# A layer-two expert program placed one edge batch further forward in a graph kernel

## The reference, cut to what matters

```
xn  = layernorm(x)
x   = x + gnn(xn) + attention(xn)       # gnn: two GAT layers, then the second one's result per node
x   = x + ffn(layernorm(x))             # ffn: 8 experts, all used, weighted by a softmax gate

gat: e = leaky_relu(el[src] + er[dst]); a = softmax of e over the edges of each dst
     out[dst] = sum of a * feat[src]
ffn: h = relu(bn(x @ W1[e] + b1)); h = relu(bn(h @ W2[e] + b2)); y = h @ Wo[e] + bo
     out = sum over e of w[e] * y[e]
```

## Time and profile before

| | us |
|---|---|
| median of 3 runs | 3636.33 (3636.3 to 3638.42) |
| the profiled execution | 3636.28 |
| its span, first to last instruction | 3634.4 |
| POOL busy in the span | 2350.2 |
| DVE busy | 2594.4 |
| PE busy | 2213.0 |
| ACT busy | 1905.4 |

### The profile page before, as it was taken

The page is one execution under the profiler, slowest core; times in us unless marked ns, Lnnn a source line. Parts: engine busy times, 40 slices in busy tenths (PEclk is TensorE's granted clock), DMA queues, the critical chain, the costliest instruction groups (busy, mean ns, idle before and its releaser), DMA issues. The chain is left out here.

```text
span 3634.4 us, 37755 instructions
## 1 busy us (share of the span) xinstructions
PE 2213.0 (61%) x8126; PEld 1372.6 (38%) x8126; DVE 2594.4 (71%) x6161; ACT 1905.4 (52%) x6135; POOL 2350.2 (65%) x2057
## 2 busy tenths in 40 slices
PE   5960044444444444544545540079999999999999
PEld 3540022232223223332323320045555555555565
DVE  8987378888888888888865643366666666666742
ACT  1210067777776667666733333256565655555642
POOL 0004788888888888888646547777777777777500
PEclk9985566666665555555567875589999999999999
DMA  6321389999999999999944435766666666666510
GB/s 189 94 74 21 115 316 348 341 342 346 343 347 338 356 371 363 362 358 369 341 156 115 114 79 170 226 196 201 199 202 200 204 201 203 199 199 199 183 44 11
DMA packets 279436, 821.07 MB, mean 226 GB/s; under 512 B 71711, under 2 KB 149135, under 8 KB 257694
## 3 DMA queue, kind: packets, MB, share of 16 engines
q0 software_dynamic: 126496, 377.09, 34.5%
q1 hardware_dynamic: 121790, 420.89, 30.4%
q10 hardware_dynamic: 30944, 20.94, 2.1%
HBM read 425.16 MB, written 394.56 MB: 226 GB/s over the span
## 5 line engine op out<-in xcount | busy, mean ns | idle before, releaser
L1323 POOL DMA_INDIRECT e_rows<-scratch_table,k_src x1680 | 1975.0, 1176 | 514.1 <-issue 345.8
L1435 ACT ACTIVATE e_rows<-e_rows,e_wr 128x64 f32<-128x64 f32 (+1 forms) x4200 | 1202.1, 367 | 3.6
L1415 DVE SCALAR_TENSOR_TENSOR e_ring<-e_ring,e_kext,e_rows 128x512 f32<-128x512 f32 (+1 forms) x1568 | 964.2, 615 | 226.1 <-ACT e_rows L1435 135.9
L2071 PE MATMUL e_p_y<-e_wfo,e_h 128*112 128x256 f32 x1792 | 418.7, 388 | 40.8 <-DVE e_y L1833 40.7
L2057 PE MATMUL e_p_b<-e_h,e_wf 128*128 128x448 f32 x896 | 374.8, 563 | 19.5 <-ACT e_h L1980 19.5
L2071 PEld LDWEIGHTS e_p_y<-e_wfo,e_h 128*112 128x112 f32 x1792 | 321.9, 181 | 152.0 <-ACT e_h L1980 60.7
L2045 PE MATMUL e_p_a<-e_xt,e_wf 128*128 128x448 f32 x896 | 358.7, 544 | 0.7 <-ACT e_xt L1995 0.7
L1980 ACT ACTIVATE e_h<-e_p_a,e_shift,e_scale 128x448 f32<-128x448 f32 x224 | 160.3, 721 | 281.6 <-PE e_p_a L2045 281.6
L978 PE MATMUL e_p_c<-e_vext,e_kphi 112*128 112x129 f32 x224 | 68.1, 458 | 374.5 <-DVE e_kphi L868 374.5
L1833 DVE SCALAR_TENSOR_TENSOR e_y<-e_p_y,e_w,e_y 112x256 f32<-112x256 f32 x448 | 194.3, 475 | 96.5 <-PE e_p_y L2071 96.4
L1383 DVE TENSOR_TENSOR e_rows<-e_rows,e_wr 128x3840 f32<-128x3840 f32 x56 | 232.6, 4153 | 13.5 <-ACT e_wr L1428 13.5
(11 more groups left out here) (393 smaller groups left out, 3763.3 us busy)
## 6 DMA issues: line engine op xcount, KB each, us to landing
scratch_sums<-e_ring SPq DMA_DIRECT2D x56, 2112.0 KB, 9.7
scratch_sums<-e_ring SPq DMA_DIRECT2D x56, 1848.0 KB, 9.4
scratch_sums<-e_ring SPq DMA_DIRECT2D x56, 1032.0 KB, 4.5
scratch_sums<-e_ring SPq DMA_DIRECT2D x56, 903.0 KB
e_rows<-scratch_table,k_src POOLq DMA_INDIRECT x1680, 4.8
scratch_table<-na_frow ACTq DMA_DIRECT2D x56, 227.5 KB, 2.3
scratch_table<-hi_frow ACTq DMA_DIRECT2D x56, 115.5 KB, 2.1
na_x<-in_x SPq DMA_DIRECT2D x7, 896.0 KB, 17.3
```

Source lines behind the costliest of these rows:

```text
L1323: nc.gpsimd.indirect_dma_start(out=rows[:, n % B, g, :], out_offset=None, in_=table, in_offset=bass.IndirectOffsetOnAxis(ap=k.src[:, n * G ...
L1415: nc.vector.scalar_tensor_tensor(ring[:, i, j - c0, 0:W], prev, kext[:, 0, j + 1:j + 2], rows[:, rb, j, 0:W], ALU.mult, ALU.add).then_inc( ...
L1435: last = nc.scalar.activation(rows[:, rb, j, at], rows[:, rb, j, at], ACT.Copy, scale=wr[:, b, h, j + 1:j + 2])
L2071: last = nc.tensor.matmul(self.p_y[bank][0:BK, i * D:(i + 1) * D], self.h2[:, e % 2, kt, v:v + BK], self.wfo[:, e, kt, :], start=kt == 0, ...
```

## The change

In the `Experts` class a constant `AHEAD = 1` is added, and `place(n)` gives (r, kq) of n + 1 instead of n. SyncE, VectorE and ScalarE use it, so each thing that the expert program does stands one batch (15 steps) sooner beside the ring steps. Some are then put at other steps: `below` goes from step 3 to step 11 of kq 2, `shares` to step 14, the joins, `spread` and `norm` to kq 3. Together `below` stands 7 ring steps sooner than before, and `norm` 11. On TensorE `turn(g)` goes behind `second_layer(f, 7)`, and `outputs(f, 6)` ahead of `first_layer(g, 0)`; the tails' matmuls, `turn_weights` and `bias` go one or two experts later. The tails' own steps on the other engines don't move. In GpSimd's order the node gathers of groups 1 to 13 stay; those of group 0 go from batch 8, steps 0 to 7, to batch 6, steps 7 to 14.

```diff
+    AHEAD = 1
+    def place(self, n):
+        return (n + self.AHEAD) // PB, (n + self.AHEAD) % PB
     def sync(self, sp, n, half):
-        r, kq = n // PB, n % PB
+        r, kq = self.place(n)
     def pool(self, pool, n, j):
-        if n % PB == 0 and n >= 2 * PB and j < 2 * KB:
+        if n == PB + 2 and j >= G - 2 * KB:
+            at = j - (G - 2 * KB)
+            self.gather(pool, 0, at // 2, at % 2)
+        if n % PB == 0 and n >= 3 * PB and j < 2 * KB:
             self.gather(pool, n // PB - 2, j // 2, j % 2)
     def vector(self, dve, n, j):
-        r, kq = n // PB, n % PB
+        r, kq = self.place(n)
...
         if kq == 2:
-            if j == 3:
+            if j == 11:
                 self.below(dve, g)
-            if j == 7:
+            if j == 14:
                 self.shares(dve, g)
-            if j in (7, 10, 11, 13):
-                self.join(dve, g, (7, 10, 11, 13).index(j))
-            if j == 14:
+        if kq == 3:
+            if j in (1, 2, 4, 5):
+                self.join(dve, g, (1, 2, 4, 5).index(j))
+            if j == 6:
                 self.spread(dve, g)
-        if kq == 3 and j == 5:
-            self.norm(dve, g)
+            if j == 9:
+                self.norm(dve, g)
     def scalar(self, act, n, j):
-        nc, r, kq = self.nc, n // PB, n % PB
+        nc, (r, kq) = self.nc, self.place(n)
+        if self.valid(g - 1) and kq == 0 and j == 0:
+            self.keep(act, g - 1, 0, 0)
...
-            if kq == 2 and j == 3:
+            if kq == 2 and j == 10:
                 self.weights(act, f)
         if self.valid(g):
-            if kq == 2 and j == 4:
+            if kq == 2 and j == 12:
                 act.wait_ge(self.d_ready, g + 1)
...
-            if kq == 3 and j == 3:
+            if kq == 3 and j == 7:
                 act.wait_ge(self.sd_asked, g + 1)
...
-            if kq == 3 and j == 8:
-                self.turned(act, g, 0)
-                self.turned(act, g, 1)
...
-        if self.valid(g) and kq == 3 and j == 13:
-            self.keep(act, g, 0, 0)
+        if self.valid(g) and kq == 3 and j == 12:
+            self.turned(act, g, 0)
+            self.turned(act, g, 1)
     def tensor(self, pe):
             for e in range(E):
-                if e == 7 and self.valid(g):
-                    self.turn(pe, g)
                 if on and e < E - 1:
                     self.first_layer(pe, f, e + 1)
-                if e == 0 and self.valid(q):
+                if e == 2 and self.valid(q):
                     tails.tensor_turn(pe, q)
-                if e == 1 and self.valid(q):
+                if e == 3 and self.valid(q):
...
-                if e == 2 and 0 <= q < Q - 1:
+                if e == 4 and 0 <= q < Q - 1:
                     tails.tensor_spread(pe, q)
-                if e == 4 and on:
+                if e == 5 and on:
                     self.turn_weights(pe, f)
-                if e == 5 and on:
+                if e == 6 and on:
                     self.bias(pe, f)
                 if on:
                     self.second_layer(pe, f, e)
-                if e == 0 and self.valid(q):
+                if e == 2 and self.valid(q):
                     tails.tensor_back(pe, q)
+                if e == 7 and self.valid(g):
+                    self.turn(pe, g)
+                if e == 0 and self.valid(o):
+                    self.outputs(pe, o, E - 1)
+                if e > 0 and on:
+                    self.outputs(pe, f, e - 1)
                 if e == 7 and self.valid(g):
                     pe.wait_ge(self.xt_ready, 2 * (g + 1))
...
                     self.first_layer(pe, g, 0)
-                if e == 0 and self.valid(o):
-                    self.outputs(pe, o, E - 1)
-                if e > 0 and on:
-                    self.outputs(pe, f, e - 1)
-                if e == 7 and self.valid(g):
                     self.gate(pe, g)
```

## The result

The changed kernel takes 3729.49 us (median of 4 runs, 3728.65 to 3733.34), the kernel before, run beside it, 3637.38 us: a ratio of 1.0253, 95% interval 1.0236 to 1.0271. Predicted were 3726 us, and slower. The profiled execution took 3733.34 us with a span of 3731.6 us, 97.2 us more than the span before. 6.3 us of these lie ahead of layer two (its first edge gather is issued at 2189.40, before at 2183.09), in work that the change doesn't touch; a second profile of the same kernel lacks them (span 3722.4, layer two from 2180.57). From layer two's first gather to the end it is 1542.2 us against 1451.3, so +90.9.

A forecast was written before the change was run, and what follows sets the result against it. It took GpSimd's stream of gathers in layer two to set the pace. Its terms, 2.5 + 83 + 5.9 + 1.5 - 3.0 = +89.9 us, on a median of 3636.33 gave 3726 us, range 3672 to 3748 (chance 0.8).

The forecast's parts named there:

- seven steps in hand: GpSimd's gathers at L: 37 ring steps ahead of VectorE, of 44 allowed without a wait; the change leaves none.
- L: The moment in each round when VectorE, idle at below for the group's last node gather, goes on.
- S: GpSimd's stall per round in layer two: 4.9 us plus 3.3 for the clock, 8.3 us with the semaphore.
- The join block: VectorE's work from below to norm, with 14 ring steps instead of 18: gather 24 stalls 4.2 us.
- TensorE behind it: From turn to first_layer(g,2), its keep and VectorE's step at p = 40: ends at L+46.3, a stall of 4.9 us.
- The clock: TensorE, idle 8 to 9 us before the turn, then runs at the lower clock: 3.3 us per round (bounds 0 and 4).
- Rival 1: TensorE's gap before the turn splits into pieces that don't lower its clock: S = 4.9, 3687 us; chance 0.20.
- What it waits it can't regain: GpSimd from L on: its issues stood back to back, so time spent waiting for VectorE is never made up.
- The bound of 1.5 us: Gathers 10 to 24: a waiting GpSimd meets less VectorE work, sparing at most 1.5 us per round; 0 was taken.
- A longer chain: Steps behind the turn wait for ScalarE's keeps and hold VectorE and GpSimd: S above 9.9, over 3748 us; chance 0.10.
- TensorE as the bound: TensorE sets the round, which would shrink to the 85.0 us that 68 gathers take: 3576 us; chance 0.06.
- Buffers that don't bind: GpSimd is nearer than counted or VectorE's 14 steps are faster: S is 0, no change, 3636 us; chance 0.04.

The follow-up runs named there:

- e6: The changed kernel with AHEAD back at 0 and the tails' matmuls back at their earlier experts; 3627.39 us, 0.9975 of the kernel before.
- e7: The changed kernel with four buffers of edge rows in layer two instead of three; 3694.40 us, 1.0164 of the kernel before.
- e10: The kernel before, with GpSimd's layer-two gathers waiting for a ring step 7 further on than the buffer needs; 3647.14 us, 1.0041 of the kernel before.
- e8: The changed kernel with 40 matmuls of 64 columns on TensorE ahead of the turn, results unused; 3699.82 us, 1.0179 of the kernel before.
- e5: The changed kernel run once more without an edit; 3729.85 us, 1.0261 of the kernel before.
- e12: e6 with 40 matmuls of 64 columns on TensorE ahead of each turn, results unused; 3640.68 us, 1.0019 of the kernel before.
- e9: The changed kernel with both four row buffers in layer two and 40 filler matmuls ahead of the turn; 3665.92 us, 1.0085 of the kernel before.
- e1: The same kernel as e6, run on another chip where the kernel before takes 3824.93 us; 3882.00 us, 1.0142 of it.

## Why the prediction was right

**GpSimd sets the pace, with seven steps in hand at L, and the change takes them.** Right. GpSimd's waits name VectorE's ring step, at L+9 to L+54, and make 105 us, where 80 to 95 were expected. That the batch forward of the expert program causes them, e6 shows (a batch later, and all of it is gone); that these waits are the three buffers' limit, e7 (none over 0.3 us left, though only 3.4 of the 8.4 us a round come back, since the wait for the tails follows); that the seven steps in hand count even where nothing else moves, e10 (1.5 us a round).

**Terms of the sum.**

| the prediction's term | predicted | measured |
|---|---|---|
| 1: group 0 waits for its tails | +2.5 | +1.0 up to L(1) (GpSimd waited 3.0, 0.3 of it issue) |
| 2: ten rounds | +83 | +84.2 (987.63 - 903.41) |
| 3: last gather round, to the end of turn 12 | +5.9 | +7.4 |
| 4: turn 12 to turn 13 | +1.5 | +1.3 |
| 5: behind the last turn | -3.0 | -3.0 (93.91 against 96.91) |
| sum | +89.9 | +90.9 |

**What S is made of.** The sum of S was right (8.3 predicted, 8.4 measured) by two errors that cancel: without the clock it was 1.4 us too low, and the clock was 1.2 us too high. That the number came so near is luck.

- The join block: 4.2 predicted. Gather 24 leaves at L+25.1 instead of L+19.5: 5.6. `norm` ended 24.4 us behind L, where the count of four ring steps fewer comes to 23.3. I didn't count that ScalarE's exponent and a keep (two instructions) now stand together in step 12, right behind L, and VectorE waits 0.9 us for the row that they hold up. The rest, some 0.3 us, lies between the end of a ring step and the gather that waited for it.

```profile
3245.12 0.48 DVE L1415 SCALAR_TENSOR_TENSOR e_ring<-e_ring,e_kext,e_rows 128x256 f32<-128x256 f32 x1 [0.91 <-ACT e_rows L1435]
```

- TensorE behind it: 4.9 predicted at p = 40. e8, with the clock kept, has gather 40 at L+47.4 against 41.4: 6.0. But the place was wrong. Gather 33 already leaves at L+37.9 in e8 and at L+40.2 in the changed kernel, before at L+31.9 (round 9 each time): 6.0 and 8.3 us late. Gather 40 waits only 0.33 us, issue included, and adds nothing. So the stall is complete at p = 33, behind the keep of first_layer(g,1), seven steps ahead of the keep of first_layer(g,2) that the prediction took. Both come from the same turn, which is why the size came out.
- The clock: 3.3 predicted, 2.1 measured by e8. The gap before the turn is one piece (9.13 us) and the clock behind it is the lower level, as said. But what runs at half speed is the turn and the sixteen output matmuls, 6.74 us instead of 4.47. The price was taken from a row with eight longer matmuls; it should have been taken from those that stand behind this gap.

By the Trainium skill, "TensorE: Matmul & The Clock Gate", section "What's actually happening", "the ramp penalty is <1% of a typical kernel span; don't fit to a specific cold count". By e5 and e8 it was 30 us of 3730, 0.8%. The size agrees, and a forecast that leaves it out for being that small misses 30 us. Rival 1, the clock that holds, is out; its 3687 us would have been wrong even so, since without the clock's part S is 6.3 and not 4.9.

**"What it waits it can't regain"** was too strong. In e10 0.8 of 2.3 us come back within the round; of the 2.7 us that group 0's tails cost, 1.0 is left at L(1); and in the changed kernel 9.5 us more of waits per round (105 by 11) make the round 8.4 us longer. The bound of 1.5 us for this was in the prediction, and I took 0. GpSimd's gathers of a round are busy 68.5 us instead of 69.6. In the kernel before, between 2450 and 3300 us, the 67 edge gathers beside which VectorE stood idle took 0.95 us on average, the 369 beside which it was busy nearly all the time 1.06. The Trainium skill, "SBUF — State Buffer", section "SBUF: two separate sides", names a port that the two share. These rows show a tie with VectorE's work; no run here shows that the port is the cause.

**The other rivals.** A longer chain (over 3748): its size is out, but its mechanism is there. The ring steps behind the keeps of steps 0 and 2 of the new group wait 4.29 and 2.37 us, and gathers 31 and 33 wait for them; it is there that S goes from 4.8 us at gather 30 to 8.3 at gather 33. It stays below 9.9. TensorE as the bound (3576): out, as the rounds grew and didn't shrink, and e6 runs its rounds in 89.1 us with TensorE busy 84. It would be one with 9 us of work more, as e12 shows. Buffers that don't bind: out by e7 and e10.

**Two slips in the prediction, without effect on its sum.** It says that VectorE waited at `below` 12 us and more in all ten rounds; it was 9.7 to 12.0 us in groups 2 to 11. And the low end of its range, 3672, is none of the bounds that it works out (3680, and 3663 with the 1.5 us spared).

**Where it stays open.** With both edits (e9) a round is still 2.7 us longer than before. GpSimd waits there for the tails, and TensorE is nearly full; which of the two would give more wasn't tried. The kernel to keep is e6, 0.25% below the kernel before (0.14 to 0.35%): all of the change but the batch forward and the later place of the tails' matmuls. Whether a smaller step forward, or `below` alone, would gain wasn't tried.

## What to carry to other kernels

Before a consumer is moved ahead, count in the trace how many steps the engine that feeds it has in hand in its buffers while the consumer waits: a consumer that waits for a transfer of that same engine gains nothing by coming sooner, and takes each step from that hand. Try the parts of a moved schedule one by one; here all but the batch forward gave 8 us together, and that one cost 100 us. When one limit is lifted, look for what stands a few us behind it before expecting the whole wait back.

## What the runs showed of the hardware

- One chip, in the one set of runs made on it, ran this layer quite differently: matmuls 2.1 to 2.8 us apart at a granted clock of 0.54, the kernel before 5% slower, and two kernels' order reversed (e1 1.4% slower than before there, 0.25% faster elsewhere). Its traces lack about half of the landings, so they can't say why. A comparison is worth only as much as the runs of the base on its own chip.
- Forty short matmuls that compute nothing, in a gap of 9 us, saved 30 us in the changed kernel. In e6, where the gap is 5.5 us and TensorE has only some 7 us a round to spare, they cost 16 us.
